# Cross attention with a ternary feed-forward block: a new order of the out projection, the query products and the small additions in each block

## The reference

```python
q, k, v = ln(x) @ Wq.T, ctx @ Wk.T, ctx @ Wv.T         # 16 heads, 8 key/value heads, 32 wide, q and k twice
w = softmax(q1 @ k1.T) - lam * softmax(q2 @ k2.T)
attn = w @ v
x = x + (attn * rsqrt(mean(attn**2) + eps) * g * (1 - LAMBDA_INIT)) @ Wo.T
h = gelu((ln(x) * ln1_g + ln1_b) @ ternary(w1).T + b1)  # hidden 2048
x = x + (ln(h) * ln2_g + ln2_b) @ ternary(w2).T + b2
```

## Time and profile before

| | |
|---|---|
| median of 3 runs | 2359.46 us (2351.84 to 2360.43) |
| profiled execution: time, span | 2361.55 us, 2359.7 us |
| PE, DVE, ACT, POOL busy | 92%, 76%, 64%, 44% |
| mean granted TensorE clock | 0.957 |

### The profile page before, as it was taken

How to read it: one execution, slowest core, us unless ns; L and a number is a source line. 1 busy time by engine, 2 the same in 40 slices (tenths; PEclk the granted TensorE clock), 3 DMA queues, 4 the chain that set the end, 5 groups by cost and what they waited for, 6 DMA issues and landing times.

```text
span 2359.7 us, 45373 instructions
## 1 busy us (share of the span) xinstructions
PE 2161.4 (92%) x18239; PEld 1182.7 (50%) x18239; DVE 1797.9 (76%) x2722; ACT 1518.9 (64%) x1973; POOL 1046.8 (44%) x803
## 2 busy tenths in 40 slices
PE   7777999999999999999999999999999999999888
PEld 5444454554545455455545545555455545555443
DVE  4677778787887878788797878879787887967763
ACT  3566575756667675666767576676757666774744
POOL 2302625527181543718164361817346281733517
PEclk9868999999999999999999999999999999999989
DMA  8323123041512303131331303232140313222010
GB/s 293 111 51 81 45 60 86 16 105 28 115 47 67 78 19 104 25 99 47 84 76 32 101 15 99 47 86 58 46 113 5 104 42 95 50 52 58 10 47 18
DMA packets 253009, 160.16 MB, mean 68 GB/s; under 512 B 171812, under 2 KB 221580, under 8 KB 252288
## 3 DMA queue, kind: packets, MB, share of 16 engines
q1 hardware_dynamic: 249792, 152.07, 25.0%
q0 software_dynamic: 3008, 5.20, 0.7%
HBM read 51.82 MB, written 20.38 MB: 31 GB/s over the span
## 4 chain that ended last, share of the span: by engine, by line
PE 56%; DVE 18%; POOL 13%; ACT 6%; issue 4%; DMA 1%; SPq 1%; POOLq 0%; DVEq 0%; ACTq 0%
POOL attn_raw L686 11%; PE ps L1616 11%; PE ps L1598 10%; PE ps L1533 4%; PE ps L1448 4%; PE ps L1450 4%; PE ps L1449 4%; PE ps L1501 4%; PE ps L1626 2%; PE ps L1562 2%; PE ps L1563 2%; ACT arena L869 2%; PE ps L1561 2%; DVE arena L1245 2%; DVE arena L1116 2%
## 5 line engine op out<-in xcount | busy, mean ns | idle before, releaser
L686 POOL TENSOR_TENSOR attn_raw<-attn_raw 128x512 f32<-128x512 f32 x448 | 627.3, 1420 | 55.0 <-ACT attn_raw L840 29.5
L1598 PE MATMUL ps<-rows,w1T 128*128 128x512 f16 x2048 | 486.7, 381 | 8.9 <-DVE rows L1240 8.9
L664 POOL TENSOR_TENSOR q<-q 128x512 f16<-128x512 f32 x128 | 197.6, 1548 | 572.7 <-ACT q L799 555.8
L1116 DVE TENSOR_REDUCE arena<-ps 128x6 f32<-128x924 f32 (+1 forms) x308 | 326.0, 1083 | 35.9 <-PE ps L1501 34.6
L1616 PE MATMUL ps<-w2T,arena 128*128 128x512 f16 x1440 | 348.9, 398 | 0.0
L1245 DVE SCALAR_TENSOR_TENSOR arena<-attn_raw,vec_cols,arena 128x512 f16<-128x512 f32 x256 | 295.2, 1157 | 40.1 <-ACT arena L838 40.0
L835 ACT ACTIVATE attn_raw<-ps,vec_cols,wstep 128x512 f32<-128x512 f32 x256 | 199.0, 777 | 194.6 <-PE ps L1598 192.2
L1598 PEld LDWEIGHTS ps<-rows,w1T 128*128 128x128 f16 x2048 | 194.1, 98 | 230.7 <-DVE rows L1240 21.2
L653 POOL TENSOR_TENSOR rstd<-var,neghalf 128x4 f32<-128x4 f32 x48 | 48.6, 1012 | 477.3 <-DVE var L1187 406.1
L1146 DVE TENSOR_TENSOR attn_raw<-arena,attn_raw 128x1024 f16<-128x1024 f32 (+1 forms) x128 | 199.5, 1589 | 54.3 <-ACT attn_raw L815 51.9
L808 ACT ACTIVATE arena<-ps 128x1024 f32<-128x1024 f32 x128 | 130.8, 1022 | 151.4 <-PE ps L1533 151.3
(11 more groups left out here) (192 smaller groups left out, 4515.4 us busy)
## 6 DMA issues: line engine op xcount, KB each, us to landing
stack_raw<-q SPq DMA_DIRECT2D x744, 64.0 KB, 2.0
arena<-in_x SPq DMA_DIRECT2D x64, 256.0 KB, 2.9
out<-arena SPq DMA_DIRECT2D x64, 256.0 KB, 2.3
arena<-in_x SPq DMA_DIRECT2D x14, 1024.0 KB, 5.9
arena<-in_L_ffn_w SPq DMA_DIRECT2D x7, 1024.0 KB, 15.5
rows<-in_x SPq DMA_DIRECT2D x2, 1024.0 KB, 7.1
stack_raw<-in_L_xattn_Wq SPq DMA_DIRECT2D x8, 256.0 KB, 10.3
k_att<-k_store SPq DMA_DIRECT2D x4, 495.0 KB
```

What stands on the lines that cost most here:

```text
L686: ins = pool.tensor_tensor(acc[:, e, :], acc[:, e, :], src[:, j % NG, :], ALU.add)
L1116: dve.tensor_reduce(negmax[:, tt:tt + 2, u0:u1], ps[:, bank:bank + 2, 0:(u1 - u0) * S].rearrange("p b (u s) -> p b u s", s=S), AX.X, ALU.m ...
L1598: ins = pe.matmul(ps[:, B_H + j % 2, :], w1T[:, k, j * P:(j + 1) * P], rows16[:, e, k, :], start=(k == 0 and e == 0), stop=(k == KD - 1 an ...
```

## The change

It has these parts:

1. `ATTEND` gets `k14 k15` behind e1: the last two `ffn_step`s of row tile 0 are done in the next block, behind the first half of row tile 1. In the last block `gelu_sums` goes ahead of the last `ffn_step`.
2. `ATTEND` gets `y3 z3` ahead of v7: DVE adds row tile 3 of block i-1 there and not in `mid_rows`. SP stores that tile and loads the residual rows of tile 2 there.
3. Before v7 PE multiplies quarter 0 only; after it quarters 1 and 2 together, then query product 4, then quarter 3, then query products 5 and 6.
4. `ln1_offsets(i+2)` moves from ahead of the first `mid` to behind the first `variances`.
5. `add_constant(i)` moves on POOL from behind the last `sum_gelu` to ahead of the first one (from block 1 on).
6. SP issues the early pairs of stacked queries at q1 and q3, ahead of t0 and t1. In block 0 it issues only pair 0 there.
7. Block 0: a new `FIRST` list, the small products for the output vectors in bank 3 one after the other, and with that row maxima of block 1 in pairs over four banks.

```diff
 ATTEND = [(w[0], int(w[1:] or 0)) for w in (
-    "c e1 g y0 y1 s0 l0 e2 q0 s1 l1 q1 s2 v0 l2 h1 s3 v1 l3 h2 t0 y2 z0 z1 s4 v2 l4 q2 z2 s5 v3 l5 q3 t1 s6 v4 l6 h3 "
-    "s7 v5 l7 h4 v6 t2 v7").split()]
+    "c e1 k14 k15 g y0 y1 s0 l0 e2 q0 s1 l1 q1 s2 v0 l2 h1 s3 v1 l3 h2 t0 y2 z0 z1 s4 v2 l4 q2 z2 s5 v3 l5 q3 t1 s6 v4 l6 h3 "
+    "s7 v5 l7 h4 v6 t2 y3 z3 v7").split()]
...
-FIRST = tokens("r1 w0 s0 l0 b0 w1 s1 l1 x1 w2 v0 w3 s2 l2 q0 w4 v1 w5 s3 l3 w6 v2 w7 s4 l4 q1 t0 w8 v3 w9 s5 l5 q2 w10 v4 s6 l6 t1 w11 v5 s7 l7 q3 w12 v6 t2 "
-               "w13 v7 w14 w15")
+FIRST = tokens("r1 w0 s0 l0 b0 w1 s1 l1 x1 w2 q0 s2 v0 l2 w3 w4 s3 v1 l3 w5 t0 q1 s4 v2 l4 w6 w7 s5 v3 l5 w8 t1 q2 s6 v4 l6 w9 w10 "
+               "s7 v5 l7 q3 w11 v6 t2 w12 v7 w13 w14 w15")
...
-            return 2 if c < 2 else 4
+            return 4 if c else 2
...
SyncE, block 0
-                        stack_queries(1, p, 0)
+                        if p == 0:
+                            stack_queries(1, 0, 0)
...
SyncE, blocks from 1
+                        elif what == "q" and n % 2 and ahead:
+                            stack_queries(i + 1, n // 2, i)
                         elif what == "t":
-                            if n == 2:
-                                load_x_res(i, TT - 2)
-                                if ahead2:
-                                    load_x_in(i + 2)
+                            if n == 2 and ahead2:
+                                load_x_in(i + 2)
                             transpose_attn(i, n)
-                            if n < 2 and ahead:
-                                stack_queries(i + 1, n, i)
                 transpose_attn(i, KD - 1)
                 if i:
-                    store(i - 1, TT - 1)
                     load_x_res(i, TT - 1)
...
                 if ahead:
-                    for p in range(QATT // 2, QM // 2):
+                    for p in range(QATT // 2 if i else 1, QM // 2):
                         stack_queries(i + 1, p, i)
...
GpSimd
                     elif what == "g" and i:
-                        add_constant(i - 1, range(TT))
+                        if i == 1:
+                            add_constant(0, range(TT))
                         power(3, s_gln, s_rstd4, i - 1)
...
+                if i:
+                    add_constant(i, range(TT))
                 for j in range(JH):
                     if j:
                         sum_gelu(i, j)
...
-            add_constant(NBLK - 1, range(TT))
             power(3, s_gln, s_rstd4, NBLK - 1)
...
VectorE, mid_rows
                 rms_variance(c)
-                if c:
-                    add_ffn(c - 1, TT - 1, ffn_bank(TT - 1))
-                    add_shift(c - 1, TT - 1)
                 if ahead2:
                     ln1_stats(c + 2)
...
+                mid(0)
+                variances(0)
                 if ahead2:
                     ln1_offsets(c + 2)
-                mid(0)
-                variances(0)
                 mid(1)
                 variances(1)
...
TensorE
                             for tt in range(TT):
-                                out_projection(i, tt, (0, 1))
+                                out_projection(i, tt, (0,))
                         values(i, n)
...
+                    elif what == "k" and i:
+                        ffn_step(i - 1, n, (2,))
...
-                for pairs in ((2,), (3,)):
-                    for tt in range(TT):
-                        out_projection(i, tt, pairs)
+                for tt in range(TT):
+                    out_projection(i, tt, (1, 2))
                 if ahead:
-                    for n in range(QATT, QEARLY):
+                    queries(i + 1, QATT)
+                for tt in range(TT):
+                    out_projection(i, tt, (3,))
+                if ahead:
+                    for n in range(QATT + 1, QEARLY):
                         queries(i + 1, n)
                 h_transposes(i)
...
-                for j in range(JH - FLAG, JH):
+                for j in range(JH - FLAG, JH - 2 if ahead else JH):
+                    if j == JH - 1:
+                        gelu_sums(i)
                     ffn_step(i, j, banks)
```

More of the change, by code:

```diff
@@ L558, in iteration @@
                         transpose_attn(0, p)
-                        stack_queries(1, p, 0)
-                    transpose_ternary(JH + 12)
+                        if p == 0:
+                            stack_queries(1, 0, 0)
                     transpose_attn(0, 2)
                     load_x_in(2)
-                    for n in range(13, JH):
+                    for n in range(12, JH):
                         transpose_ternary(JH + n)
@@ L1052, in output_vectors @@
                     dve.wait_ge(s_lnrow, 1)
-                    dve.tensor_copy(ln2_rows, ps[0:4, 1, :]).then_inc(s_lncopy, 1)
+                    dve.tensor_copy(ln2_rows, ps[0:4, 3, :]).then_inc(s_lncopy, 1)
                 elif j == VECTORS_AT[4]:
                     dve.wait_ge(s_spread, 1)
-                    dve.tensor_copy(g2_row[:], ps[:, 0, :]).then_inc(s_rows, 1)
-                    dve.scalar_tensor_tensor(out_const[:], ps[:, 1, :], wstep[:, 1:2], out_const[:], ALU.mult,
+                    dve.tensor_copy(g2_row[:], ps[:, 3, :]).then_inc(s_rows, 1)
+                elif j == VECTORS_AT[6]:
+                    dve.wait_ge(s_spread, 2)
+                    dve.scalar_tensor_tensor(out_const[:], ps[:, 3, :], wstep[:, 1:2], out_const[:], ALU.mult,
                                              ALU.add).then_inc(s_rows, 1)
@@ L1120, in row_maxima @@
             def row_maxima(c, tbs):
-                if c < 2:
+                if c == 0:
                     for tb in tbs:
@@ L1433, in output_vectors @@
                     pe.wait_ge(s_l2, 2)
-                    wait(pe, s_q32, 1, QM, QM)
                     for n in range(JH):
-                        ins = pe.matmul(ps[0:4, 1, :], ln2_16[:, :, :, n].rearrange("p e h -> p (e h)"), w2T[:, n, :],
+                        ins = pe.matmul(ps[0:4, 3, :], ln2_16[:, :, :, n].rearrange("p e h -> p (e h)"), w2T[:, n, :],
                                         start=(n == 0), stop=(n == JH - 1))
                     ins.then_inc(s_lnrow, 1)
-                elif j == VECTORS_AT[3]:
-                    pe.wait_ge(s_lncopy, 1)
-                    pe.wait_ge(s_pick, 3)
-                    for e in range(2):
-                        ins = pe.matmul(ps[:, e, :], pick[:, e, :], ln2_rows, start=True, stop=True)
-                    ins.then_inc(s_spread, 1)
+                elif j in (VECTORS_AT[3], VECTORS_AT[5]):
+                    e = int(j == VECTORS_AT[5])
+                    if e:
+                        pe.wait_ge(s_rows, 1)
+                    else:
+                        pe.wait_ge(s_lncopy, 1)
+                        pe.wait_ge(s_pick, 3)
+                    pe.matmul(ps[:, 3, :], pick[:, e, :], ln2_rows, start=True, stop=True).then_inc(s_spread, 1)
             def split_product(dst, w_hi, w_lo, r_hi, r_lo, first, last):
@@ L1496, in row_scores @@
                 if tb >= row_banks(c):
-                    wait(pe, s_tmax, c, NT, tb - row_banks(c) + (1 if c < 2 else 2 - tb % 2))
+                    wait(pe, s_tmax, c, NT, tb - row_banks(c) + (2 - tb % 2 if c else 1))
                 elif tb == 2:
@@ L1709, in _ @@
                 iteration(i)
-            gelu_sums(NBLK - 1)
     return nc
```

2 lines of the change are left out of this document (1 added, 1 removed).

## The result

The changed kernel took 2410.45 us (median of 4 runs, 2409.81 to 2412.63) against 2356.9 for the kernel before on the same chip: a ratio of 1.0233, 95% interval 1.0218 to 1.0249. It is slower, as forecast, but by 53.5 us where 27 were forecast (2386), and 2 us above the range.

The account below looks back on a forecast made before the run. Two chains on other engines were taken to bound the kernel (value product 7 to `hidden(0)`, then POOL's sums to `gelu_sums`), PE only filling them. Blocks +51 and edges -24 gave +27 on 2361.55, as a median 2386 us; range 2347 to 2408.

Parts of the forecast that it names:

- Edges: Block 0 and the blocks from 14 to the end: together -24 us, from -12 to -34, with two terms of -5 early in block 0.
- The sum of a block: Blocks 1 to 13: 1.1 us more without clock falls, 3.9 us a block with them, 51 us over 13.
- PE's wait ahead of `gelu_sums`: End of the feed-forward stage: one 4.1 us wait, with a clock fall behind it in nearly every block, 1.7 us.
- the gain is zero as long as POOL bounds: Steps k14 and k15: moving them replaces two waits by one of 4.1 us and gains nothing.
- Quarter 2: Projection: PE idles 2.5 us for its transpose behind the 1 MB load, which cannot go earlier; clock fall there 1.0 us.
- Offsets: DVE, behind the first `mid` and `variances`: 1.65 us later, delaying `hidden(0)`; costs 1.65 us a block, from 1.2 to 3.0.
- rival (a): Quarter 2's transpose does not wait for the 1 MB load; block costs 0.3 us, kernel 2339 us; chance 0.12.
- `add_constant`: POOL, ahead of the first `sum_gelu`: four additions take 5.5 us, 0.35 is caught up, 0.75 arrives at `gelu_sums`.
- The fall at query product 7: Clock fall behind PE's wait before the last xhats, slowing query product 7: 0.1 us a block.
- (b): Rival for the whole kernel: the clock holds, giving -10 us, 2350; chance 0.10.
- (d): Rival: the offsets' move does nothing because ACT is not on the path, 21 us less, 2365; chance 0.10.
- (c): Rival: the edges bring only -12 us or all clock falls come, 2398 to 2420; chance 0.11.

Follow-up runs that it names:

- a_old_first: Changed kernel with the old `FIRST` list on all engines, SP's list of block 0 as changed: ratio 1.0140 to the kernel before.
- a_sp_order: Changed kernel with SP's ternary transposes in block 0 reordered to fit the new `FIRST` (0-5, 6-8, 9-11 ahead of quarters 0, 1, 2): ratio 1.0185.
- a_offsets_first: Changed kernel with `ln1_offsets` back ahead of the first `mid`: ratio 0.9924 to the kernel before.
- b_k14: Kernel before with only the last two feed-forward steps (k14, k15) moved behind the maxima and the second half of row tile 1: ratio 1.0197.
- a_no_k14: Changed kernel with feed-forward steps 14 and 15 back ahead of `gelu_sums`: ratio 1.0051 to the kernel before.
- b_offsets_late: Kernel before with only `ln1_offsets` moved behind the first `mid` and `variances`: ratio 1.0091.
- a_const_late: Changed kernel with `add_constant` back behind the last `sum_gelu`: ratio 1.0141 to the kernel before.
- a_fill: Changed kernel plus 16 matmuls with discarded result ahead of `gelu_sums`, while PE waits for POOL: ratio 1.0062 to the kernel before.
- best3: Changed kernel with offsets first, constants late, SP's block 0 order mended, and steps 14 and 15 back ahead of `gelu_sums`: ratio 0.9696, 2285.7 us.
- best1: Changed kernel with `ln1_offsets` ahead of the first `mid`, `add_constant` behind the last sum and SP's block 0 order mended: ratio 0.9819, 2325.0 us.

## Why the prediction was wrong in size

**The step that failed** is "Edges", and in it the two terms for the first part of block 0: "pair 1 goes behind, and with the offsets 3 us later I count -5" and "The list `FIRST` puts each score ahead of the values before it, as `ATTEND` does: -5". Instead of -10 up to `hidden(0)` it was +6.6. I followed PE's list alone and did not ask which signs SP's transposes wait for, and what stands behind these on SP. With the other edges (-5.7 measured against -24 in all) that is 18 of the 26.5 us that are missing. The blocks add 4 (55.0 against 51), and the medians differ by 4 more than the spans of the two profiled executions. That the new list is at fault in that place is shown by a_old_first, and that it acts through SP's order by a_sp_order; each gives back 9 us. That is not the whole of the gap: with either one `hidden(0)` of block 0 is 2.2 to 2.6 us earlier than in the kernel before, where 10 had been forecast. The later offsets have a part in it, since a_offsets_first gives back 5.9 us at this place; how the three share the gap is open. The other edges had the right sign: the feed-forward stage of block 0 (-5.9 for -5), block 14 (-4.0 for -5), block 15 (-1.7 for -2.5), the end (-0.7 for -1.8).

**The sum of a block (3.9 forecast, 4.2 measured) was right by luck: its errors cancel.**

- PE's wait ahead of `gelu_sums`: 4.1 forecast, 4.00 measured, and its cause as forecast. The fall of the clock behind it was under-sized. I took 1.7 from two blocks, each with a stretch of 3.4 us at half clock; behind the merged wait it was 6.83 in most, and in block 6 9.78 - 6.45 = 3.3 us were lost. I had written of the merged wait "the gain is zero as long as POOL bounds", and looked there for a gain only; the part's real price is 46 us, shown by b_k14 and, in the changed kernel, some 43 by a_no_k14.
- Quarter 2: 2.5 us of PE idle forecast, 0.32 measured, so also no fall of the clock there (1.0 in my sum). "The load ... cannot go earlier" was wrong: SP was late with stacked pair 1, which the change moves.
- Offsets: 1.65 forecast. Alone in the kernel before it is 1.6 a block (b_offsets_late), but my way to it went over the late quarter 2, which did not come. In the changed kernel the first `mid` came at 15.6 behind value product 6 (17.7 forecast, 19.2 before), and the offsets, with their inputs at hand, stood behind it: the new order's gain was thrown away at that place. That reading rests on the timelines; no run has the old projection together with the offsets first. So rival (a) was half right: PE came 2 us earlier, through the early load and not through a transpose that overtakes it; and the block did not gain by it.
- `add_constant`: 0.75 forecast, 1.6 measured (52.87 against 51.25; a_const_late gives 1.65 back). The four took 5.84 rather than 5.5, `q_lo(7)` was 0.46 later, and the catching up of 0.35 was not there. The estimate of 5.1 that I had derived from the Trainium skill, GPSIMD Engine Reference, section 1 (Specifications), was too low. Its rule on which VectorE instructions contend is borne out: the second and the fourth addition start while a VectorE instruction with two SBUF inputs is running and took 1.71 us each, the first and the third start beside a reduction from PSUM and took 1.27, no more than alone.
- The fall at query product 7: forecast at 0.1 a block, seen in block 6 at 3.40 us of half clock; some of it is in the 14.1 - 13.3 = 0.8 from offsets to `hidden(0)`.

**The rivals.** (b), the clock holds, fell: half clock rose from 6.0 to 11.6 us a block. (d), the offsets' move does nothing, fell: both experiments show a price. (c) was nearest, by its first half: the edges brought 5.7 where (c) said 12. Its range ended at 2420 and I cut it off at 2408 because of its chance of 0.11.

**How far the accounts close.** Before to changed: half of the added 5.5 us at half clock is 2.8 a block, POOL's later sums are 1.6, together 4.4 for 4.2 measured. The 1.6 holds for the model block; over all 13 blocks `gelu_sums` is only 1.2 later, since half clock ahead of it had cost some of them time before. The later offsets don't appear as a term: in block 6 they come 73.4 us behind `gelu_sums` where it was 70.6, and 3.3 of that was lost by query product 0 already, so behind it the earlier first `mid` and their later place about cancel. The Trainium skill, in TensorE: Matmul & The Clock Gate, Terms, has this measure: the penalty is about the throttled time times the share of the clock that is held back. The traces here agree to within half a microsecond a block: 2.8 for 3.3 in b_k14, and 3.15 for 2.8 in a_fill. The prices of the parts are not additive: undone one at a time in the changed kernel, the offsets (73), steps 14 and 15 (43) and the constants (22) would give 138 us, but best3, with all three undone and SP's order mended besides, is 127 below (1.0233 - 0.9696 of 2357). What remains open is why the same kind of wait is followed by 3.4, 6.8 or 10.2 us at half clock. It doesn't go by the length of the wait alone: it was 10.24 behind 3.37 in b_k14 and in most blocks 6.83 behind 4.00 in the changed kernel, and in a_const_late all three follow a wait of 3.37. In that run it goes with the moment at which the clock falls: the earlier, counted from `gelu_sums`, the longer it stays at half. What sets that moment the runs don't show.

## What to carry to other kernels

Where PE waits on another engine's chain anyway, leave real work between its short waits: the move that "cost nothing" because POOL bounds made one long wait out of three and by itself cost 46 us, where the whole change cost 53.5. When an engine's work is reordered, follow the queue behind it (here SP's transposes of block 0) to the item that each waits for, before a gain is booked. And when a step is made earlier, look whether the work that should profit by it stands behind something else: with the offsets in front of the first `mid` the changed kernel was 4.9 us a block shorter, where the same move was worth 1.6 in the kernel before. That the earlier value product 7 makes this difference is read from the timelines and not shown by a run.

## What was unexpected of the hardware

- The time at half clock behind one wait took three lengths, 3.41, 6.83 and 10.24 us, even in one kernel and behind the same wait of 3.37 us (a_const_late). The longest began 0.5 to 1.2 us before `gelu_sums`, the shortest 1.8 to 1.9 us behind its start.
- Sixteen discarded matmuls in a block made the kernel 40 us faster; ten of them took best1 from 0.9819 to 0.9687.
- POOL's four additions of 128x512 took 4.94 us beside a nearly idle DVE and 5.84 us in their new place. The longer time is in two of the four: those that start while DVE works on two inputs in SBUF took 1.71 us, those that start beside its reductions from PSUM 1.27. It is so in each of blocks 1 to 14 of the changed kernel. The last two in block 6, and the DVE instruction ahead of the slow one:

```profile
1095.34 1.27 POOL L670 TENSOR_TENSOR arena<-arena,out_const 128x512 f32<-128x512 f32 x1
1096.57 1.71 POOL L670 TENSOR_TENSOR arena<-arena,out_const 128x512 f32<-128x512 f32 x1
1096.23 0.92 DVE L1243 SCALAR_TENSOR_TENSOR arena<-attn_raw,vec_cols,arena 128x512 f16<-128x512 f32 x1
```
